# The feed-forward mask of a decoder layer, added on the tensor engine instead of multiplied on the vector engine

## The reference

```python
inter = xf @ c1_w.T @ c2_w.T                 # rank 16, 3584 scores for each row
blk = inter.reshape(B * T, 56, 64)
idx = jnp.argmax(blk, axis=-1) + jnp.arange(0, 3584, 64)     # first maximum of each block of 64
h = relu(einsum('bkm,bm->bk', w1[idx], xf))
out = einsum('bk,bkm->bm', h, w2t[idx])
```

## Time and profile before

| | us |
|---|---|
| median of 3 runs | 846.73 (845.98 to 847.13) |
| the profiled execution | 849.98 |
| its span | 848.2 |
| PE busy in the span | 819.0 (97%) |
| DVE, ACT, POOL busy | 514.4, 232.4, 251.3 |
| one turn of the loop over groups | 91.47 |

### The profile page before, as it was taken

How to read it: one execution, slowest core, us unless ns; L and a number is a source line. 1 busy time by engine, 2 the same in 40 slices (tenths; PEclk the granted TensorE clock), 3 DMA queues, 4 the chain that set the end, 5 groups by cost and what they waited for, 6 DMA issues and landing times.

```text
span 848.2 us, 10814 instructions
## 1 busy us (share of the span) xinstructions
PE 819.0 (97%) x3928; PEld 660.3 (78%) x3932; DVE 514.4 (61%) x812; ACT 232.4 (27%) x324; POOL 251.3 (30%) x120
## 2 busy tenths in 40 slices
PE   4999998989899999999999999999999999999998
PEld 4988976457688888878887888888888888778886
DVE  4555799999957842676248823784268624882222
ACT  5456526673320231021201231013202220123100
POOL 2844488515510242013401241024202340134100
PEclk9999999999999999999999999999999999999999
DMA  8126401001310112002200031012200230012022
GB/s 339 40 96 202 149 1 53 10 5 63 100 50 12 51 57 93 12 25 74 99 12 25 25 99 49 12 49 74 74 12 25 74 99 0 25 29 94 0 100 99
DMA packets 16791, 53.20 MB, mean 63 GB/s; under 512 B 3200, under 2 KB 3456, under 8 KB 16640
## 3 DMA queue, kind: packets, MB, share of 16 engines
q1 hardware_dynamic: 16624, 51.85, 18.0%
q10 hardware_dynamic: 144, 1.05, 0.4%
HBM read 48.70 MB, written 4.19 MB: 62 GB/s over the span
## 4 chain that ended last, share of the span: by engine, by line
PE 86%; DVE 11%; ACT 1%; DMA 1%; issue 1%; POOL 0%; SPq 0%; ACTq 0%; DVEq 0%
PE bank L1191 15%; PE bank L1192 15%; PE bank L1193 15%; PE bank L1372 12%; PE bank L1373 12%; PE bank L1374 12%; DVE stats L798 2%; PE bank L1348 1%; PE bank L1337 1%; DVE x L914 1%; DVE xT_lo L827 1%; DVE xn L893 1%; DMA W_raw<-wqkv 1%; DVE pick L964 1%; DVE pairs L1055 1%
## 5 line engine op out<-in xcount | busy, mean ns | idle before, releaser
L472 POOL TENSOR_TENSOR w_lo<-w_raw,w_hi 128x1024 fp32r<-128x1024 f32 x56 | 141.0, 2531 | 471.3 <-ACT w_hi L601 471.3
L1372 PE MATMUL bank<-w_hi,h_hi 128*128 128x512 f32 x448 | 177.6, 396 | 0.0
L1191 PE MATMUL bank<-xT_hi,w_hi 128*128 128x512 f32 x448 | 176.5, 394 | 0.0
L1192 PE MATMUL bank<-xT_lo,w_hi 128*128 128x512 f32 x448 | 175.1, 391 | 0.0
L1193 PE MATMUL bank<-xT_hi,w_lo 128*128 128x512 f32 x448 | 175.0, 391 | 0.0
L1374 PE MATMUL bank<-w_hi,h_lo 128*128 128x512 f32 x448 | 174.7, 390 | 0.0
L1373 PE MATMUL bank<-w_lo,h_hi 128*128 128x512 f32 x448 | 174.6, 390 | 0.0
L972 DVE SCALAR_TENSOR_TENSOR bank<-bank,maskT 128x512 f32<-128x512 f32 x56 | 38.9, 698 | 155.1 <-PE bank L1193 153.4
L987 DVE TENSOR_TENSOR x<-bank,x 128x512 f32<-128x512 f32 x112 | 76.8, 688 | 76.6 <-PE bank L1374 75.2
L608 ACT ACTIVATE maskT<-bank 128x512 bf16<-128x512 bf16 x56 | 33.5, 597 | 291.3 <-PE bank L1348 291.3
L1193 PEld LDWEIGHTS bank<-xT_hi,w_lo 128*128 128x128 f32 x448 | 84.5, 189 | 17.7
(11 more groups left out here) (142 smaller groups left out, 962.7 us busy)
## 6 DMA issues: line engine op xcount, KB each, us to landing
w_raw<-w SPq DMA_DIRECT2D x56, 512.0 KB, 3.3
x<-x_in SPq DMA_DIRECT2D x8, 512.0 KB, 10.5
ctx_raw<-ctx_in SPq DMA_DIRECT2D x8, 512.0 KB, 3.7
xn<-ctx_in SPq DMA_DIRECT2D x8, 512.0 KB, 5.2
out<-x SPq DMA_DIRECT2D x7, 512.0 KB, 2.6
W_raw<-wqkv SPq DMA_DIRECT2D x6, 512.0 KB, 10.1
c_raw<-c SPq DMA_DIRECT2D x56, 32.0 KB, 1.8
Wo_raw<-wo ACTq DMA_DIRECT2D x1, 1024.0 KB, 4.7
```

The costliest lines, as they stand in the source:

```text
L472: nc.gpsimd.tensor_tensor(lo, raw, hi.bitcast(F32), ALU.subtract).then_inc(w_lo_done, 1)
L1191: nc.tensor.matmul(dst, ah, bh, start=n == 0, stop=False)
L1192: nc.tensor.matmul(dst, ah, bl, start=False, stop=False)
L1372: nc.tensor.matmul(dst, h_hi[:, j, m], w2_hi[:, j, c], start=j == 0, stop=False)
```

## The change

The picks are stored for all row tiles of a group, negated (`not_equal` in place of `is_equal`: 1 where a unit was not picked). There is no transpose, no `maskT`, and no `relu_mask`. Instead, after the 24 matmuls of a (j, half), four more matmuls of 128 columns with the stored picks as weights and an identity times -2^120 (`floor_b`) as moving operand add -2^120 to the bank wherever a unit was not picked (`hidden_mask`). ACT's `h_hi` becomes a Relu, which turns those into zero, and DVE's `h_lo` becomes max(·, 0) - h_hi. There are two score banks (6 and 7) used in turn, each released by the finished pick, and the second block maximum is kept in the score bank itself. `u_stack` is written hi by ACT for all partitions, and DVE then overwrites two of the four partition quarters with the lo part. In group 0 the row biases on POOL are split around two weight cuts, and the table of what stands between the products is new.

```diff
+    floor_b = small("floor_b", [P, P], BF16)
-        score_bank = bank[6]
+        score_bank = [bank[6], bank[7]]
+        cmax = [b[:, 0:GH // BLK] for b in score_bank]
...
-            for t in range(NT):
+            for t in range(3):
                 add_rowbias(t)
-            for i in range(2, NW):
+            cut_w(0, 2)
+            for t in range(3, 5):
+                add_rowbias(t)
+            cut_w(0, 3)
+            for t in range(5, NT):
+                add_rowbias(t)
+            for i in range(4, NW):
                 cut_w(0, i)
...
-            def copy_maskT(g, t):
...
+            def hi_u(b):
+                if b == 0:
+                    act.wait_ge(mm_done, nth("U", 0) + 1)
+                else:
+                    act.wait_ge(u1_done, 1)
+                nc.scalar.activation(u_stack[:, b * SB:(b + 1) * SB], u_bank[b][:, :], ACT.Copy).then_inc(u_hi_done, 1)
             def hi_h(g, j, half):
-                act.wait_ge(relu_masked, g * 2 * GJ + (hidden_pos(g, j, half) + 1))
+                act.wait_ge(mm_done, hidden_nth(g, j, half) + 1)
                 nc.scalar.activation(h_hi[:, j, half * SB:(half + 1) * SB], bank[2 * (j % 2) + half][:, :],
-                                     ACT.Copy).then_inc(h_hi_done, 1)
+                                     ACT.Relu).then_inc(h_hi_done, 1)
...
+            def lo_u(b):
+                dve.wait_ge(u_hi_done, b + 1)
+                for q in (1, 3):
+                    quarter = slice(32 * q, 32 * q + 32)
+                    lo = u_stack[quarter, b * SB:(b + 1) * SB]
+                    ins = nc.vector.tensor_tensor(lo, u_bank[b][quarter, :], lo.bitcast(F32), ALU.subtract)
...
-                link(nc.vector.tensor_reduce(cmax[:, :], cd, AX.X, ALU.max), off)
...
-                nc.vector.tensor_tensor(pk, cd, cmax[:, :].rearrange("p (b o) -> p b o", o=1).to_broadcast(wide),
-                                        ALU.is_equal).then_inc(pick_ready, 1)
+                link(nc.vector.tensor_reduce(cm, cd, AX.X, ALU.max), off)
+                nc.vector.tensor_tensor(pk, cd, cm.rearrange("p (b o) -> p b o", o=1).to_broadcast(wide),
+                                        ALU.not_equal).then_inc(pick_ready, 1)
...
+            def hidden_mask(g, j, half):
+                dst = bank[2 * (j % 2) + half]
+                pe.wait_ge(pick_ready, g * NT + TB * (half + 1))
+                for i in range(TB):
+                    last = nc.tensor.matmul(dst[:, i * P:(i + 1) * P], pick[:, TB * half + i, j * P:(j + 1) * P],
+                                            floor_b[:, :], start=False, stop=i == TB - 1)
+                last.then_inc(mm_done, 1)
...
+            hidden_products(0, 0, 0, within({4: [(score_tile, 0)], 5: [(score_tile, 1)]}))
+            hidden_products(0, 1, 0, within({4: [(score_tile, 2)]}))
+            rank_projection(1, within({1: [(score_tile, 3)]}))
+            hidden_products(0, 0, 1, within({5: [(hidden_mask, 0, 0), (hidden_mask, 1, 0)]}))
+            hidden_products(0, 1, 1, within({0: [(score_tile, 4)], 1: [(score_tile, 5)], 4: [(score_tile, 6)]}))
+            hidden_products(0, 2, 0, within({1: [(score_tile, 7)]}))
+            hidden_mask(0, 2, 0)
+            hidden_products(0, 3, 0, within({2: [(hidden_mask, 0, 1), (hidden_mask, 1, 1)]}))
+            hidden_mask(0, 3, 0)
+            hidden(0, 2, 1)
+            hidden(0, 3, 1)
```

More of the change, by code:

```diff
@@ L313, in hidden_pos, with products_nth @@
             return (HIDDEN_0 if isinstance(g, int) and g == 0 else HIDDEN).index((j, half))
+        def products_nth(g, j, half):
+            return g * 2 * GJ + (PRODUCTS_0 if isinstance(g, int) and g == 0 else HIDDEN).index((j, half))
         def prev_unit_on(b):
@@ L738, in _ @@
             hi_w(0, 1)
-            for t in range(3):
-                copy_maskT(0, t)
             hi_w(0, 2)
             hi_w(0, 3)
-            copy_maskT(0, 3)
+            hi_u(1)
             hi_h(0, 0, 0)
@@ L748, in _ @@
             hi_w(0, 5)
-            copy_maskT(0, 4)
             hi_w(0, 6)
[L751 to L757, removed]
-            with act.Fori(0, NG - 1) as g:
[L760 to L765, removed]
+            hi_h(0, 2, 0)
+            hi_h(0, 0, 1)
+            hi_h(0, 1, 1)
+            hi_w(0, 7)
+            hi_h(0, 3, 0)
+            hi_h(0, 2, 1)
+            hi_h(0, 3, 1)
+            with act.Fori(0, NG - 1) as g:
+                hi_w(g, NW)
+                hi_w(g, NW + 1)
                 hi_w(g + 1, 2)
                 hi_w(g + 1, 3)
-                copy_maskT(g + 1, NT - 1)
                 both(hi_h, g + 1, 0)
@@ L1167, in _ @@
                 for j, half in HIDDEN:
-                    relu_mask(g + 1, j, half)
                     lo_h(g + 1, j, half)
@@ L1192, in split_mm @@
                     nc.tensor.matmul(dst, ah, bl, start=False, stop=False)
-                    last = nc.tensor.matmul(dst, al, bh, start=False, stop=n == len(pairs) - 1)
+                    last = nc.tensor.matmul(dst, al, bh, start=False, stop=n == len(pairs) - 1 and not open_ended)
                 return last
@@ L1330, in score_tile, with hidden_products @@
                         pe.wait_ge(u_stacked, 1)
-                    else:
-                        pe.wait_ge(score_read, t)
+                        pe.wait_ge(bank_free, nth("U", 0) + 1)
+                    if t >= 2:
+                        pe.wait_ge(pick_ready, t - 1)
                     if t == TB:
-                        pe.wait_ge(u_stacked, 2)
+                        pe.wait_ge(u_stacked, 3)
                 else:
-                    pe.wait_ge(score_read, g * NT + t)
-                nc.tensor.matmul(score_bank[:, :], u_stack[:, t * P:(t + 1) * P], c2_stack[:, :],
+                    pe.wait_ge(pick_ready, g * NT + (t - 1))
+                nc.tensor.matmul(score_bank[t % 2][:, :], u_stack[:, t * P:(t + 1) * P], c2_stack[:, :],
                                  start=True, stop=True).then_inc(score_done, 1)
-            def transpose_pick(g, t):
-                pe.wait_ge(pick_ready, g * NT + (t + 1))
-                if isinstance(g, int) and g == 0:
-                    if t > 0:
-                        pe.wait_ge(maskT_copied, t)
-                else:
-                    pe.wait_ge(maskT_copied, g * NT + t)
-                for j in range(GJ):
-                    last = nc.tensor.transpose(maskT_bank[:, j * P:(j + 1) * P], pick[:, j * P:(j + 1) * P], id_b[:, :])
-                last.then_inc(maskT_done, 1)
-            def hidden(g, j, half, between=lambda n: None):
+            def hidden_products(g, j, half, between=lambda n: None):
                 b = 2 * (j % 2) + half
@@ L1363, in hidden @@
                          for k in range(KD)]
-                split_mm(bank[b][:, :], pairs, between).then_inc(mm_done, 1)
+                split_mm(bank[b][:, :], pairs, between, open_ended=True).then_inc(products_done, 1)
+            def hidden_mask(g, j, half):
[5 more added lines that the diff above has]
+                last.then_inc(mm_done, 1)
+            def hidden(g, j, half):
+                hidden_products(g, j, half)
+                hidden_mask(g, j, half)
             def unit_part(u, js):
```

131 lines of the change are left out of this document (36 added, 95 removed).

## The result

Measured side by side, the kernel before has a median of 846.93 us (845.98 to 847.36, 4 runs) and the changed one 852.97 us (851.21 to 853.43, 4 runs), ratio 1.0065 [1.005, 1.008]: 6.0 us slower, outside the predicted range. The profiled execution of the changed kernel took 853.43 us, its span 851.6, with the granted clock at 1.0 throughout.

What follows compares the result with a forecast made beforehand. PE was taken to bound the kernel, busy for all 91.47 us of a loop turn, with at most 5.2 us winnable in group 0. Loop zero plus group 0 +0.9 on 846.73 gave 847.6 us, range 843.2 to 850.5.

Steps and rivals of the forecast that it cites:

- The four DVE and ACT edits in the loop ... zero: Loop: relu_mask and mask copies gone, Relu for Copy, fused lo part only shorten engines PE does not wait for; zero.
- my rivals: Picks slip past weight cuts (842.8 to 844.8, chance 0.28); masks dearer (851.8, 0.13); group 0 stalls grow (849.3, 0.11).
- I take 0.30 as before, a difference of zero: Loop on PE: a mask group costs about 0.30 us like a transpose group; ends 0 and +18 us over 56 groups.
- of 91.3 to 91.6 us: Loop: expected length of a turn in the profile after, with PE busy throughout.
- PE starts 1.0 us late: Group 0 start: first hidden product waits for u's lo part, until 196.0 instead of 194.99.
- 1.0 + 1.7 + 2.2 + 1.3: Group 0 stalls of PE: start, pick 3 at first masks, pick 4 at score 6, pick 7; 6.2 us in all.
- the first rival: Group 0: picks slip past POOL's weight cuts, wholly or half; 842.8, with half of the gain 844.8; chance 0.28.
- Outputs starting near 253.3: End of group 0: outputs start at 252.5 + 1.0 - 0.2 = 253.3.
- The sum for group 0: Group 0: stalls 6.2 us against 5.2 before with its slow clock, masks in pairs -0.2; +0.6 to +1.2, middle +0.9.
- which I had half counted: Group 0: a clock drop behind the 2.2 us wait (1.7 us), mostly hidden by the pick 7 stall; +0.5.
- The exposed instruction freed: Group 0 picks beside POOL: last instruction always 0.69 us; `cand*order` still exposed, 1.5 to 2.5 in three or more of eight.
- The prediction's estimate from that figure: Picks reading PSUM: each would grow by some 0.13 us, about 1 us over the eight; nothing was added for it.

Runs made afterwards that it cites:

- e2: Changed kernel, but in the loop ACT waits for output unit 4 before copying the next group's first two weight tiles; 846.75 us, ratio 0.9985.
- e3: Kernel before, with ACT's first two weight copies for the next group put ahead of the mask copies; 857.4 us, ratio 1.0115.
- e4: Changed kernel, order kept, but c2 is first copied into a score bank and the subtraction reads it from there; 847.32 us, ratio 0.999.
- e7: e2 with every group of four mask matmuls issued twice; 860.48 us, ratio 1.0148.
- e10: e2 repeated unchanged, in the same comparison as e9; 847.85 us, ratio 0.9998.
- e5: e2 with u cut and stacked on DVE as in the kernel before; 846.07 us, ratio 0.9975.
- e8: e2 with group 0 tuned: POOL's cuts 4 and later wait until pick 4 is through, score 7 and second masks later; 846.53 us, ratio 0.9982.
- e9: The edits of e5 and e8 together, loop as in e2; 843.96 us, ratio 0.9958.
- e1: Kernel before, unchanged, profiled and timed once more; 848.37 us, ratio 1.0001.
- e6: e2 with all eight row biases first on POOL, ahead of the third weight cut, as in the kernel before; 847.71 us, ratio 0.9988.

## Why the prediction was wrong

- **"The four DVE and ACT edits in the loop ... zero" is the step that failed.** I asked only what delay on DVE the picks could bear (more than 5 us) and looked at the engines whose work shrank. I did not ask what the removed mask copies had been holding back on ACT. They held the weight copies 22 us away from `cut_c2`; without them POOL's cut falls upon it, DVE's instruction goes from 0.69 to 2.84 us, and since the score behind it has only 1.56 us of slack for these 2.15 us, it costs 0.88 us a turn: 5.3 of the 6.0 us. Shown by e2 (taken out), e3 (put into the kernel before) and e4 (the second SBUF input alone). It was none of my rivals, though the mechanism stood in the text for group 0, and though the order of ACT's list was there to be read.
- **"I take 0.30 as before, a difference of zero", a turn "of 91.3 to 91.6 us": the part on the masks was right.** 0.21 to the next start and 0.32 behind, as measured in the earlier trace rows; e7 gives 0.058 us for each. Without the collision a turn is 91.46.
- **"PE starts 1.0 us late":** it waited 0.93, and counted from the last transposes it starts 1.17 later (3.15 us behind them, 1.98 before). Two 32-partition subtractions took 1.41 for the 1.38 taken; ACT's copy 0.57 for 0.6. Right within 0.2 us.
- **Stalls "1.0 + 1.7 + 2.2 + 1.3":** measured 0.93, 0, 2.25, 1.30. Three sizes are right; the wait of 1.7 at the first masks did not come, since the third weight tile was issued late and pick 1 slipped past the cut, half of the first rival. (In the profiles of e2 and e4, with the same group 0, a wait of 0.35 and of 0.53 stands there.) I had let POOL's cut follow its row biases with no regard for SP's list, in which the transfer ahead of ACT's copy stands behind those of c2: the same omission as in the loop, an order on an engine that nobody seemed to wait for.
- **"Outputs starting near 253.3":** 250.50. Of the 2.8 us, 1.23 came from an earlier start, the rest from the missing 1.7. The sum for group 0 was +0.9 and would have been about -0.8 by this pair of profiles, and the clock did not fall, which I had half counted. A timing settles this only within a microsecond: e2 and e10 have the loop of before and stand at 0.9985 and 0.9998.
- **The exposed instruction freed:** the last pick instruction always at about 0.69, right; `cand*order` at 1.49, 1.93, 2.20 and 2.61, four of eight, right.
- The two parts, +5.3 from the loop and -0.2 to -1.3 from the rest (the ratios of e10 and e2), sum to 4.0 to 5.1 us, against a measured ratio whose interval runs from 4.2 to 6.8 us. What lies between that sum and the 6.0 of the medians is not resolved.

## What to carry to other kernels

When an instruction disappears from an engine that nobody waits for, read what stood behind it in that engine's list: it now runs earlier, and so does what it releases on the next engine. For each such step lay its new time beside the DVE instructions with two SBUF inputs that have little slack to PE; here one wait on an idle engine was worth 5.3 us. And in a start-up stretch with several waits, single removals are hard to tell from nothing (e5 and e8 stand at 0.9975 and 0.9982, the kernel that they are built on at 0.9985 and 0.9998); the two together (e9) stand clear of it, 3.9 us below e10. That they are worth more together than their sum is not shown.

## What the runs showed of the hardware

- The half-clock stretches come and go between executions of one program, and how often they come depends on the program. The kernel before fell in group 0 in both profiles, near 148 us in one of two; of its 73 timed executions beside e1 to e10 only 2 show a mean granted clock of 1.00, of the 23 of e2 and e10, one kernel, 7 show 1.00 and 12 more 0.999. A wait of PE of 2.2 us at the score tile stands in the changed kernel, e2, e4, e6, e7 and e10; behind it the clock kept 1.00 in the profiles of all but e7, where it was 0.67 and 0.50 in the next 4 us. e5 fell to 0.50 behind a wait of 2.1 us that ended at 218.6 (steps of 1 us, columns as in the earlier trace rows):

```profile
218.00:219.00 1.00, 0.38 (x2) 0.33 (x3) 1.00 (x2) 0.00 (x0) 1.00 (x1) 1.00 0.79 262
219.00:220.00 1.00, 1.00 (x5) 0.77 (x4) 0.93 (x3) 0.00 (x0) 0.34 (x1) 0.62 0.62 250
220.00:221.00 1.00, 1.00 (x4) 0.81 (x3) 0.97 (x2) 0.00 (x0) 0.00 (x0) 0.50 0.50 152
```

- A collision costs POOL as well: a pair of cuts takes 5.19 us with a held DVE instruction beside it, 4.75 with none.
- The number of partitions does not count for DVE: 32 x 512 takes 0.70 (two in 1.41), 64 x 512 0.69, 128 x 512 0.69. Nor does a source in PSUM: the subtraction of `cut_c2` takes 0.69 from SBUF and 0.69 from a bank (e4). The Trainium skill, "VectorE: DVE Perf Modes", section "The TRN2 errata", has 62 cycles more for a PSUM source; no run here shows them. The prediction's estimate from that figure, 0.13 us for each pick, was also twice too large: of the instructions of a pick only the last has a source that moved to PSUM (`L945`).
